# One program block for cross attention and the expert layer, and another order of layer 2's work around its modulation

## What is computed

```
attn = jax.nn.softmax(jnp.clip(q @ k * scale), axis=-1)      # 16 heads, 77 keys
x = layernorm(x + (attn @ v) @ Wo + bo)                       # cross attention
logits = xf @ Wg                                              # expert layer, 16 experts
_, topi = jax.lax.top_k(logits, 2)
gates = softmax over the two chosen
y = sum over experts e: gates[:, e] * (silu(xf @ W1[e] + b1[e]) * (xf @ W11[e] + b11[e]) @ W2[e] + b2[e])
z = silu(xf @ Ws1 + bs1) * (xf @ Ws11 + bs11) @ Ws2 + bs2      # shared expert, all rows
x = layernorm(x + y + z)
```

## Time and profile before

| | |
|---|---|
| median of 3 runs | 573.44 us (572.16 to 573.55) |
| the profiled execution | 572.52 us, of which the traced span is 570.7 us |
| busy over the span | PE 471.5 us (83%), DVE 417.5 (73%), ACT 274.8 (48%), POOL 251.8 (44%) |
| mean granted TensorE clock | 0.896 of full speed |

### The profile page before, as it was taken

How to read it: one execution, slowest core, us unless ns; L and a number is a source line. 1 busy time by engine, 2 the same in 40 slices (tenths; PEclk the granted TensorE clock), 3 DMA queues, 4 the chain that set the end, 5 groups by cost and what they waited for, 6 DMA issues and landing times. The chain is left out here.

```text
span 570.7 us, 13045 instructions
## 1 busy us (share of the span) xinstructions
PE 471.5 (83%) x4676; PEld 361.8 (63%) x4676; DVE 417.5 (73%) x1416; ACT 274.8 (48%) x669; POOL 251.8 (44%) x293
## 2 busy tenths in 40 slices
PE   3888692799599787799899899798999789589993
PEld 1565552586468666677694667665577645289983
DVE  4699959788997956765788899995688648147743
ACT  4599870431213354455403768552354322458741
POOL 3643499466912103365202434350686135526650
PEclk9979785589799886899999999979998979979998
DMA  8300004330000015507000000000663201241113
GB/s 243 134 2 1 2 1 149 70 117 2 2 0 1 1 44 147 106 1 145 8 1 0 2 3 2 2 3 2 249 256 99 58 0 39 71 131 49 48 52 102
DMA packets 28001, 33.44 MB, mean 59 GB/s; under 512 B 4961, under 2 KB 21073, under 8 KB 27426
## 3 DMA queue, kind: packets, MB, share of 16 engines
q1 hardware_dynamic: 26002, 29.13, 17.6%
q0 software_dynamic: 1504, 3.15, 1.7%
q10 hardware_dynamic: 432, 0.33, 0.3%
HBM read 26.44 MB, written 6.16 MB: 57 GB/s over the span
## 5 line engine op out<-in xcount | busy, mean ns | idle before, releaser
L2166 POOL TENSOR_TENSOR ea_scaled_rows<-ea_scaled_rows 128x768 f32<-128x768 f32 (+2 forms) x21 | 24.0, 1142 | 47.2 <-ACT ea_scaled_rows L2081 46.1
L3799 POOL DMA_INDIRECT em_results<-em_y_slot,slot_rows x31 | 29.7, 958 | 28.7 <-DVE em_y_slot L3926 28.1
L317 ACT ACTIVATE norm_log<-norm_mean_var,norm_eps 128x4 f32<-128x4 f32 x20 | 5.9, 296 | 66.3 <-DVE norm_mean_var L279 66.3
L3658 PE MATMUL banks<-em_slotT,em_weights 128*128 128x128 f32 x248 | 35.2, 288 | 2.6 <-ACT em_weights L3547 2.6
L3917 DVE SCALAR_TENSOR_TENSOR em_innerT<-banks,em_bias_of,em_soft 128x128 f32<-128x128 f32 x62 | 18.9, 346 | 22.7 <-ACT em_soft L3741 20.1
L3658 PEld LDWEIGHTS banks<-em_slotT,em_weights 128*128 128x128 f32 x248 | 32.4, 204 | 3.3 <-issue 3.3
L38 PE MATMUL banks<-ea_w_high,ea_x_high 128*128 128x384 f32 x64 | 26.9, 421 | 8.0 <-DVE ea_acc L2257 8.0
L2081 ACT ACTIVATE ea_scaled_rows<-banks,ea_gate 128x192 f32<-128x192 f32 x64 | 23.3, 418 | 19.3 <-PE banks L38 19.1
L2861 POOL TENSOR_TENSOR ga_sums<-ga_sums 128x512 f32<-128x512 f32 x8 | 9.1, 1134 | 44.5 <-DVE ga_sums L2921 44.5
L3741 ACT ACTIVATE em_soft<-banks,em_bias_of 128x128 f32<-128x128 f32 x62 | 19.4, 363 | 12.1 <-PE banks L3658 12.1
L38 PE MATMUL banks<-ea_w_low,ea_x_high 128*128 128x384 f32 x64 | 23.5, 367 | 0.0
(11 more groups left out here) (519 smaller groups left out, 1524.1 us busy)
## 6 DMA issues: line engine op xcount, KB each, us to landing
em_up<-in_em_up SPq DMA_DIRECT2D x3, 1536.0 KB, 12.0
ea_wide<-ea_gates SPq DMA_DIRECT2D x4, 1024.0 KB, 11.6
em_down<-in_em_down SPq DMA_DIRECT2D x3, 768.0 KB, 13.4
em_slots<-slot_rows SPq DMA_DIRECT2D x1, 2108.0 KB, 10.3
w_qkv<-in_w_qkv SPq DMA_DIRECT2D x1, 1536.0 KB, 7.5
slot_rows<-em_slots SPq DMA_DIRECT2D x1, 1360.0 KB, 9.3
cos_half<-in_cos_half SPq DMA_DIRECT2D x1, 1024.0 KB, 7.1
sin_half<-in_sin_half SPq DMA_DIRECT2D x1, 1024.0 KB, 9.3
```

What stands on the lines that cost most here:

```text
L2166: step(pool.tensor_tensor(scaled_rows[:, k, 0:n], scaled_rows[:, k, 0:n], scaled_rows[:, k, n:2 * n], ALU.add))
L3658: ins = pe.matmul(s.ps[:, k * P:(k + 1) * P], weights[:, n % NW, k // 2, k % 2 * P:(k % 2 + 1) * P], slotT[:, n], start=True, stop=True, s ...
L3799: pool.indirect_dma_start(core.results[:, :], bass.IndirectOffsetOnAxis(ap=slot_rows[:, s, P:P + 1].bitcast(U32), axis=0), y_slot[:, s % N ...
```

## The change

It has two parts. First, cross attention no longer opens a block: it returns five functions, one for each engine, which the expert layer's block calls first, so that the meeting of all engines between the two layers is gone. DVE marks each finished row tile of x with a semaphore, `rows_ready`. PE turns half 0 of x behind the projection of tile 6 and makes its logits behind the projection of tile 7; three unread products are left instead of four. Half 1 is turned two tiles at a time, each pair with a bank and a copy of its own. DVE takes the maxima of half 0 before the logits of half 1, and POOL does its constants and half 0's copies as soon as it can. Tiles that are now written early (`em_xT`, `em_sent` and others) get a place of their own.

Second, in layer 2 POOL masks tile 3 before it averages tile 2, averages tile 3 before the affine step, and does the skip path right behind the scaling; DVE does the first round of tile 5's `select` before the film; the film products of tiles 2 and 3 get banks 3 and 4; and two of eight unread products go.

```diff
-    plan = ["taps", "norm_cols", "b1", "kernel_re", "kernel_im"] + work[0]["mean"] + work[0]["film"]
+    plan = ["taps", "norm_cols", "b1", "kernel_re", "kernel_im"] + work[0]["mean"] + work[0]["film"][:3]
     ring.update(core.ring.plan(plan, (6, 7)))
+    ring.update(core.ring.plan(work[0]["film"][3:], (3, 4)))
...
-                    short_unread(ring[f"c{b}"].ps, 8)
+                    short_unread(ring[f"c{b}"].ps, 8 if b else 6)
...
-            for g in range(NT):
-                if g < NT - 1:
-                    two["weigh"](g)
...
+            for g in range(HT):
+                two["weigh"](g)
+                if g == HT - 1:
+                    two["average"](HT - 2)
+                    two["average"](HT - 1)
                     two["affine"](0)
...
+                two["shift"](g + 1)
+                if g < HT - 2:
                     two["average"](g)
...
+            two["weigh"](HT)
+            for b in range(B):
+                two["bias"](b)
+            two["scale"](0)
+            two["skip"](0)
+            two["shift"](HT + 1)
+            two["average"](HT)
+            two["weigh"](HT + 1)
+            two["affine"](1)
+            two["shift"](HT + 2)
...
             two["select"](4)
+            two["select"](5, range(1))
             two["film"](0)
-            two["select"](5)
+            two["select"](5, range(1, K_TOP // 8))
...
+                if (stage, g) == ("project", NT - 2):
+                    turn_next(pe)
+            logits_next(pe)
+            keep_busy(pe, x, 3)
-                keep_busy(pe, x, 4)
...
+            copy_next(act)
             core.norm.act(act, step)
...
-                        core.norm.dve(dve, step, res[:, hb], out[:, hb])
+                    core.norm.dve(dve, step, res[:, hb], out[:, hb], ready=core.rows_ready)
...
+                front["tensor"](pe, first_turn, first_logits)
+                for k in range(2):
+                    s = ring[f"xT1_{k}"]
+                    s.claim(pe)
+                    for i in range(2):
+                        n = HT + 2 * k + i
+                        pe.wait_ge(core.rows_ready, n + 1)
+                        ins = pe.transpose(s.ps[:, i * P:(i + 1) * P], x[:, n], ident[:, :])
+                    ins.then_inc(s.filled, 1)
+                s = ring["logit1"]
+                s.claim(pe)
+                for k in range(2):
+                    ring[f"xT1_{k}"].taken(pe)
+                    ins = logits(range(HT + 2 * k, HT + 2 * k + 2))
...
+                    pool.wait_ge(core.rows_ready, HT * (b + 1))
+                    for k in range(2):
+                        pool.tensor_copy(sent[:, half(b), k, 0:P], x[:, half(b)]).then_inc(side_ready, 1)
```

More of the change, by code:

```diff
@@ L1698, in _ @@
             two["shift"](0)
[L1699 to L1720 removed]
+            for g in range(HT):
[3 more added lines that the diff above has]
+                    two["average"](HT - 1)
+                    two["affine"](0)
+                two["shift"](g + 1)
+                if g < HT - 2:
+                    two["average"](g)
+            two["weigh"](HT)
[8 more added lines that the diff above has]
+            two["shift"](HT + 2)
+            two["average"](HT + 1)
+            two["weigh"](HT + 2)
+            for n in range(2):
+                two["split"](n)
+            two["shift"](HT + 3)
             two["split"](2)
@@ L3056, in sem @@
         def sem(name):
-            return ctx.enter_context(nc.semaphore("ca_" + name))
+            return core.late.enter_context(nc.semaphore("ca_" + name))
         ident = t["ident"]
@@ new lines, in tensor, with scalar, exp, turn @@
+            stages = {"score": score, "first values": first_values, "last values": last_values, "turn": turn, "sum": total,
+                      "project": project, "queries": queries, "bias": turned_bias}
+            for stage, g in order():
+                stages[stage](g)
+                if (stage, g) == ("project", NT - 2):
+                    turn_next(pe)
+            logits_next(pe)
+            keep_busy(pe, x, 3)
+        def scalar(act, copy_next):
+            step = core.steps(act, "act")
+            load_exp_and_log(act)
+            for b in range(B):
+                s = ring[f"xT_{b}"]
+                s.ready(act)
+                act.copy(xT[:, half(b)], s.ps[:, :]).then_inc(s.drained, 1)
+                s = ring[f"q_{b}"]
+                s.ready(act)
+                act.activation(qT[:, half(b)], s.ps[:, :].rearrange("p (i t) -> p i t", i=HT), ACT.Identity,
+                               bias=bias["bq"]).then_inc(s.drained, 1)
+            def exp(g):
+                act.wait_ge(shifted, g + 1)
+                p = prob[:, g % AHEAD, 0:FLAT]
+                act.activation(p, p, ACT.Exp).then_inc(exps, 1)
+            def turn(g):
+                if g >= 2:
+                    ring[f"o_{g - 2}"].ready(act)
+                for n in range(3):
+                    s = ring[f"t{n}_{g}"]
+                    s.ready(act)
+                    last = min(4 * n + 4, CHUNKS)
+                    act.copy(probT[:, g % 2, 4 * n:last], s.ps[:, 0:(last - 4 * n) * P]).then_inc(s.drained, 1)
+            for g in range(2):
+                exp(g)
+            turn(0)
+            exp(2)
+            for g in range(NT):
+                if g + 1 < NT:
+                    turn(g + 1)
+                if g + 3 < NT:
+                    exp(g + 3)
+                if g == HT:
+                    core.norm.act(act, step)
+            copy_next(act)
+            core.norm.act(act, step)
+            core.keep("act", step)
@@ L3415 @@
+        return {"sync": sync, "tensor": tensor, "scalar": scalar, "gpsimd": gpsimd, "vector": vector}
 HE = 256
@@ L3425, with expert_mlp @@
 WARM = 7
-def expert_mlp(core, x, out):
+def expert_mlp(core, x, out, front):
     nc = core.nc
```

565 lines of the change are left out of this document (263 added, 302 removed).

## The result

The changed kernel takes 565.37 us in the median of 4 executions (562.62 to 567.82), beside 573.5 us of the kernel before on the same chip: a ratio of 0.987, 95% interval 0.982 to 0.991. Measured again beside the last experiments it took 567.07 us (6 executions, 564.23 to 572.01) against 574.12, the same ratio of 0.987 (0.981 to 0.993). The forecast was 565.0.

A forecast was written before the change was run, and what follows sets the result against it. The path was taken to run through the border's logits, mask, count and POOL's transfers, and through DVE in layer 2. Gains of 5.3 + 2.8 = 8.1 us from 572.52 give 564.4, as a median 565.0 us, range 562.0 to 568.5.

The forecast's parts named there:

- The border: Between cross attention and the expert layer: 4.9 us sooner at the maxima plus 0.45 at the count, 5.3 us.
- The last row to the maxima: At the start of the expert layer: 2.5 us from x's last row tile to DVE's maxima instead of 7.4.
- rival 1: Before the expert layer's count: PE's clock stays at 1.2 GHz, gain 7.0 us in all, 566.4 us; chance 0.15.
- the count: Behind the mask in the expert layer: shared expert's four passes done before the mask, so 0.45 us gained.
- The sum's bounds of 4.1 and 5.6: Limits in us around the 5.3 us gain forecast between cross attention and the expert layer.
- the cold stretch behind it: PE after its wait for the sorted rows: clock 0.50 from 497.70 to 507.00, no gain or loss booked.
- Layer 2: Fewer DVE waits and two fewer unread products bring the return transform forward by 2.8 us, bounds 1.9 and 3.3.
- the unread products: Before layer 2's film products on PE: two of eight go, worth 0.45 us.
- The margin of POOL's mask of tile 5: In layer 2: mask ready at 142.6, 0.6 us ahead of DVE, so DVE's 0.88 us wait goes.
- The return transform starting at 148.0: In layer 2 on PE: sign that the forecast is right, a start at about 148.0 instead of 150.88.
- The port pair: In layer 2: DVE's combining and POOL's instructions block each other at SBUF, gain 1.2 us instead of 2.8.
- Rival 2: Layer 2's gain is given back by a return transform at low clock: 567.2, as a median 568.0; chance 0.14.

The follow-up runs named there:

- late_half0: The changed kernel with half 0's turn, copy and logits put back behind the last row of x: 570.61 us, ratio 0.995 to the kernel before.
- layer2_only: The kernel before with just the layer 2 edits put in: 570.54 us against 573.03, ratio 0.997.
- one_turn: The changed kernel with half 1 turned as four tiles at once, with one copy and one set of logits: 566.66 us, ratio 0.988 to the kernel before.
- late_round: The changed kernel with tile 5's first select round put back behind the first film products: 567.84 us against 574.59 for the kernel before, ratio 0.988.
- after_again: The changed kernel with nothing altered, run again with the last experiments: 567.07 us against 574.12 for the kernel before, ratio 0.987.

## Why the prediction was right

**The border, 5.3 us: right, 5.5.** The last row to the maxima was put at 2.5 us and took 2.21: the two copies were put one behind the other until 1.06 us behind the last row, but took about 0.44 us each, the first begun ahead of it, and ended at 0.80. The first line of its reading, that nearly all of the 7.40 us went for half 0's turn, holds as far as late_half0 shows: 3.7 of the 5.2 us gained in C. The clock stayed high, so rival 1 (7.0 us in all, 566.4) fell; the count waits for the mask (0.87 us) and not for the shared expert's passes, and gave 0.30 us where 0.45 was booked. The sum's bounds of 4.1 and 5.6 also hold against the other profile with the old border, layer2_only, where C was 6.38 us since its second logits happened to run at 2.4 GHz: from there the gain is 4.5 us, and by time it is 4.1. Not foreseen, and seen only in the expectations for late_half0 and one_turn, is how the gain divides: 2.2 and 0.4 us were expected for half 0's early turn and the pairs, and 4.7 and 1.4 (C and D) were found. The 4.72 us wait of PE and the cold stretch behind it were forecast and came (8.70 us at clock 0.51).

**Layer 2, 2.8 us: right in its mechanism, somewhat too small by the stretches.** By time it is 2.5 us, within 0 to 3.5. B, from the film products on, is 2.8 us shorter in six of eight profiles with all of the edit (33.68 to 33.74 against 36.43 and 36.53), and A, ahead of them, about 0.8 us (a median of 24.0 against 24.8) where 0.45 had been booked for the unread products. Three of DVE's waits are gone and the film instructions run as one. The margin of POOL's mask of tile 5 was put at 0.6 us and is 140.07 - 139.64 = 0.43. The early round was booked whole and is worth 0.9. The return transform starting at 148.0 can't be read from the absolute time: measured from the norm column products it starts 1.03 + 2.57 = 3.6 us sooner (forecast 2.9). Of that, 2.57 us lie behind the start of the film products, where the forecast had 2.4, so what it lacked lies ahead of them, in A, which moves by as much without any edit.

**The port pair.** The sum by the Trainium skill's rule (SBUF — State Buffer, Who interferes with whom) was 1.2 us for layer 2. The two combining instructions did stretch beside POOL: they take 1.98 us together, 1.86 before and 1.49 in late_round. So the trace agrees with the rule in kind, as before, but the change added 0.1 us to it and not 1.6.

**Rival 2, a return transform that gives it back:** the transform took 8.87 us at a clock of 0.81 (before 9.41). It is a matter of chance by some tenths: after_again has 10.20 us at 0.69, and even that is 0.8 us longer than before, not 2.8; there B is 34.75 us, still 1.7 below the kernel before.

**The whole.** That 565.0 came so close is partly luck. The sum of 8.1 us meets the first pair of medians exactly and the second, 7.1, by a microsecond. The stretches A to D of the profiled pair give 9.4 us, of which 1.0 hangs on the second logits of the kernel before, slow in its profile and not in layer2_only's; single executions of the changed kernel lie between 562.62 and 572.01.

## What to carry to other kernels

A boundary between two program blocks costs less for the meeting itself (0.55 us here) than for the work that it keeps from moving up (3.7 us in C): list what stands behind it and needs only old data, and run the rest by pieces as its inputs finish. A duration in a trace may be that of two records for one instruction; count the records against the program before multiplying. And where two profiles differ ahead of the first edit, cut them into stretches between the same two pieces of work, and compare those over several kernels, before giving any microsecond to a cause.

## What the hardware did that I had not expected

Profiles of the same code differ in steps at fixed places. TensorE stands still for 1.4 to 1.8 us without a releaser once or twice within 256 small products (the two fences above). The last 32 products take 3.81 us in 7 of the 14 profiles and 5.37 to 5.44 in the others, behind a wait of 0.3 to 0.7 us in all of them. PE's timeline of after_again:

```profile
553.77 5.44 PE L3729 MATMUL banks<-em_y_back,em_spread_share 128*128 128x128 f32 x32 [0.31 <-DMA em_y_back<-em_results]
```

and of after:

```profile
548.87 3.81 PE L3729 MATMUL banks<-em_y_back,em_spread_share 128*128 128x128 f32 x32 [0.33 <-DMA em_y_back<-em_results]
```

The same code, with a wait that differs by 0.02 us, runs at one clock or the other, 1.6 us apart. What decides it, no run here shows.
